# The first attention of a decoder layer with one product of query and key weights instead of two projections

## The chip, the cores and the metric

The kernel runs on one core of one Trainium2 chip. The core has five engines that run their own streams of instructions and meet at semaphores: TensorE (matmuls, PE in the profile), VectorE (DVE), ScalarE (ACT), GpSimd (POOL) and SyncE (SP), which here issues DMA transfers. The metric is the device time of one execution of the whole kernel in microseconds; lower is better. SBUF is the memory on the chip that the engines read; PSUM holds what TensorE writes, in 8 banks.

## What is computed

A decoder layer over x of 4 batches of 512 rows and 256 columns: a causal attention with one head, a second attention with 16 heads whose keys and values come from a context, and a mixture of 8 experts; each adds to its input and is followed by a layer norm. The part that the change touches is the first attention:

```python
q = x @ Wq + bq
k = x @ Wk + bk
v = x @ Wv + bv
att = jnp.einsum('bqd,bkd->bqk', q, k) * scale
att = jnp.where(causal, -jnp.inf, att)
att = jax.nn.softmax(att, axis=-1)
out = jnp.einsum('bqk,bkd->bqd', att, v)
return out @ Wo + bo
...
x = _layernorm(x + _L0_attn_ref(x, ...), axis=-1)
x = _layernorm(x + _L0_xattn_ref(x, ctx_1024, ctx_1024, ...), axis=-1)
x = _layernorm(x + _L0_ffn_ref(x, ...), axis=-1)
```

## The kernel before

All data is float32. Where accuracy matters, a factor is kept as two parts, high and low (`lo_of` makes the low one), and a product is three matmuls (`mm3`, L239): high by high, high by low, low by high. In names, `a_s` is the split transposed x, `c_s` the split transposed context, `W_s` the split weights, `k_s` and `q_s` the keys and queries of the second attention on their way to DRAM, `X` the rows of the residual, `ps` the PSUM.

A batch is 4 tiles of 128 rows (NT) and two blocks of 128 columns (KD). The work goes in bodies, one for each batch b; body 0 and body 3 are written out, 1 and 2 are one loop (Fori) on every engine. A body is: `half`, the scores of the second attention of batch b for one half of the heads; `glue_and_attention1`, which ends the batch b - 1 (g) and computes the whole first attention of batch b + 1 (n); the other `half`; and `project2`, the projections of batch b + 1 for the second attention. A prologue brings in the weights and does the first attention of batch 0. After the bodies come the shared MLP, the routing, the experts and the last norm, from about 390 us on. Each engine runs its instructions in the order in which they are written; semaphores (`s["name"]`) alone tie the engines together.

In the glue (by the lines of the profile) TensorE runs: keys of the first attention, `projected` 0 and 1 (12 matmuls of 128x512, L239 `a_s,w_s`); aug transposes (L1355); transposes of the outputs, `turn_out` (L1600); queries, `projected` 2 and 3; behind cb_out the rows of values times output weights, `rows_of(0, ...)` (24 of 128x256); the turn of the second attention's combined output (L1336); scores of the first attention (L239 `c_s,q_s`, with a mask matmul L1418); the output projection of the second (24 of 128x256, `w_s,a_s`, whose `a_s` now holds the turned output); transposes of the probabilities (L1428); and PV (30 of 128x256, `v_s,pT_s`). VectorE runs the aug operations (L1071 to L1079), the copies and low parts, `combine` (L1104 to L1115, which reads the PSUM banks of the outputs, and counts cb_out), `maximum` (L981), `residual2` (L938) and `turned` (low parts of pT_s, L865). ScalarE makes the exponents and the high parts. GpSimd splits x and the context (L401 the high part, L404 the low one) and adds the bias to the values of the second attention (`v_aug`, L485). The raw context lies in `c_raw`, which also holds the values that L485 reads (`v_wait`); so SP loads the next context behind v_set, at the end of its queue of stack loads (`q_stack<-augT` L300, `k_stack<-k_rows` L283, twelve `q_stack<-q_rows` L294, `c_raw` L330).

## Time and profile before

| | us |
|---|---|
| three runs | 865.03, 865.67, 866.78 |
| median | 865.67 |
| profiled execution | 866.4 |
| its span, from the first to the last instruction | 864.6 |
| TensorE busy | 770.9 (89%) |
| VectorE, ScalarE, GpSimd busy | 404.8, 354.7, 240.6 |

The mean granted clock of TensorE is 0.957 of its upper level, 2.4 GHz. The prologue ends at 53 us; the glues stand at 66 to 88 us (body 0), 142 to 169 (body 1), 224 to 251 (body 2), 306 to 323 (body 3); the last body's work ends at about 390.

A timeline row reads: start, busy time, engine, line, operation, written tensor <- read tensors, form, and how many of one kind stand there; in brackets the engine's idle time ahead and what ended it. PE rows are matmuls, PEld rows the loads of their stationary factor, which overlap them.

### The profile page before, as it was taken

How to read it: one execution, taken by the hardware profiler on the slowest of the kernel's cores; microseconds unless marked ns; L12 is line 12 of the kernel's file. 1: busy time of each engine (PE TensorE's matmuls, PEld its weight loads, DVE VectorE, ACT ScalarE, POOL GpSimd, SP SyncE). 2: the span in 40 equal slices, each digit the busy share in tenths (PEclk: the TensorE clock that was granted, in tenths of full speed). 3: DMA queues.
4: the chain of work that ended last, by engine and by line, in shares of the span. 5: the costliest groups of instructions: out<-in, count | busy, mean ns of one | idle time of the engine just before them, and what ended most of it. 6: DMA issues, size and time to landing. Idle time of an engine off the chain costs nothing. (4 is left out here: it accounts for less than half of the span.)

```text
span 864.6 us, 15341 instructions
## 1 busy us (share of the span) xinstructions
PE 770.9 (89%) x4898; PEld 584.7 (68%) x4899; DVE 404.8 (47%) x763; ACT 354.7 (41%) x914; POOL 240.6 (28%) x262
## 2 busy tenths in 40 slices
PE   6889999899999989964899989999999999999920
PEld 4757676867777666554899966677677667767710
DVE  4565877687768757235744522122212212221216
ACT  2223655366546726604544303433433343343313
POOL 5860231141123012023277751111111111111116
PEclk9988999999999999985999999999999999999975
DMA  9945041404312440007511164410010101111034
GB/s 298 203 135 101 1 138 28 75 6 133 64 36 56 154 77 1 5 1 249 209 55 55 56 176 164 150 36 30 30 36 30 36 31 36 30 30 36 19 138 165
DMA packets 54292, 71.57 MB, mean 83 GB/s; under 512 B 14992, under 2 KB 40464, under 8 KB 53360
## 3 DMA queue, kind: packets, MB, share of 16 engines
q1 hardware_dynamic: 50848, 61.75, 26.4%
q0 software_dynamic: 3408, 9.34, 3.0%
q8 instruction: 23, 0.38, 0.2%
q14 instruction: 13, 0.11, 0.0%
HBM read 47.67 MB, written 22.88 MB: 82 GB/s over the span
## 5 line engine op out<-in xcount | busy, mean ns | idle before, releaser
L1745 PE MATMUL ps<-we,hT 128*128 x624 | 142.8, 382 | 2.5 <-ACT hT L819 2.5
L1745 PEld LDWEIGHTS ps<-we,hT 128*128 128x128 f32 x624 | 119.7, 192 | 35.5 <-issue 20.9
L1725 PE MATMUL ps<-we,xT 128*128 x312 | 140.6, 593 | 1.9 <-issue 1.9
L1263 DVE COPY hp<-ps 128x512 f32<-128x512 f32 x78 | 50.3, 686 | 158.4 <-PE ps L1725 158.4
L1059 DVE TENSOR_REDUCE mx<-ps 128x4 f32<-128x512 f32 (+1 forms) x128 | 103.9, 821 | 30.6 <-PE ps L1557 29.1
L819 ACT ACTIVATE hT<-ps,b1T 128x128 f32<-128x128 f32 x312 | 85.3, 386 | 35.1 <-PE ps L1736 35.1
L1725 PEld LDWEIGHTS ps<-we,xT 128*128 128x128 f32 x312 | 56.2, 190 | 58.1 <-issue 58.1
L607 ACT ACTIVATE xT<-ps 128x256 f32<-128x256 f32 x39 | 15.0, 386 | 180.4 <-PE ps L1708 180.4
L1557 PE MATMUL ps<-k_stack,q_stack 96*128 96x256 f32 (+1 forms) x256 | 73.1, 372 | 5.6 <-issue 1.7
L721 ACT ACTIVATE pT<-ps 128x256 f32<-128x256 f32 x128 | 49.4, 386 | 61.2 <-PE ps L1573 52.3
L583 POOL CAST yidx<-meta 128x1 int32 (+1 forms) x39 | 7.2, 185 | 238.5 <-ACT yw L828 238.5
L1557 PEld LDWEIGHTS ps<-k_stack,q_stack 96*128 96x128 f32 x256 | 40.4, 199 | 33.8 <-issue 23.2
L724 ACT ACTIVATE pT<-ps 128x256 f32<-128x256 f32 (+1 forms) x128 | 62.5, 489 | 0.0
L1271 DVE TENSOR_TENSOR ysum<-ps,b2b 128x256 f32<-128x256 f32 x39 | 16.6, 425 | 95.2 <-PE ps L1745 95.2
L239 PE MATMUL ps<-xT_s,ws_s 128*128 128x256 f32 x384 | 49.6, 291 | 11.0 <-DVE xT_s L865 9.2
L239 PEld LDWEIGHTS ps<-xT_s,ws_s 128*128 128x128 f32 x384 | 48.6, 200 | 11.7 <-issue 11.7
L239 PE MATMUL ps<-ws_s,h_s 128*128 128x256 f32 x384 | 47.9, 284 | 0.0
L239 PEld LDWEIGHTS ps<-ws_s,h_s 128*128 128x128 f32 x384 | 46.5, 191 | 0.5 <-DVE ws L1183 0.5
L586 POOL DMA_INDIRECT pair_out<-yw,yidx x39 | 38.3, 983 | 29.6 <-POOL yidx L583 29.6
L1579 PE MATMUL ps<-q_stack,k_stack 98*128 98x256 f32 (+1 forms) x128 | 46.3, 362 | 0.0
L1736 PE MATMUL ps<-ident,hp 128*128 128x128 f32 x312 | 40.5, 273 | 1.4 <-DVE hp L1263 1.4
L239 PE MATMUL ps<-a_s,w_s 128*128 128x512 f32 x144 | 38.1, 412 | 2.9 <-DVE a_s L865 1.5
(221 smaller groups left out, 1202.0 us busy)
## 6 DMA issues: line engine op xcount, KB each, us to landing
we<-in_w SPq DMA_DIRECT2D x16, 1024.0 KB
k_stack<-k_rows SPq DMA_DIRECT2D x24, 256.0 KB, 4.8
slot_rows<-attn SPq DMA_DIRECT2D x1, 4992.0 KB, 25.0
xs<-slot_rows SPq DMA_DIRECT2D x39, 128.0 KB, 2.0
k_rows<-k_s SPq DMA_DIRECT2D x16, 256.0 KB, 3.1
yl<-pair_out SPq DMA_DIRECT2D x4, 1024.0 KB, 8.8
q_stack<-q_rows SPq DMA_DIRECT2D x48, 64.0 KB, 5.7
x_raw<-in_xT SPq DMA_DIRECT2D x4, 512.0 KB, 5.5
```

Source lines behind the costliest of these rows:

```text
L239: m = nc.tensor.matmul(out, lhs(a), rhs(b), start=first and n == 0, stop=last and n == 2, skip_group_check=check)
L586: pool.indirect_dma_start(out=pair_out, out_offset=bass.IndirectOffsetOnAxis(ap=yidx[:, q, :], axis=0), in_=yw[:, q, :], in_offset=None).t ...
L721: nc.scalar.activation(pT[:, m % 2, u % 2, 0:2 * P], ps[:, bank, 256:512], ACT.Exp, scale=SCALE2)\
L724: nc.scalar.activation(pT[:, m % 2, u % 2, 2 * P:2 * P + w], ps[:, bank + 1, 0:w], ACT.Exp, scale=SCALE2).then_inc(s["b_exp"], 1)
L819: last = nc.scalar.activation(hT[:, c, :], ps[:, 4 + c // 4, (c % 4) * P:(c % 4 + 1) * P], ACT.Gelu, bias=b1T[:, bass.ds(e * NH + c, 1)])
L1059: nc.vector.tensor_reduce(mx[:, n, 2 * p:2 * p + 2, r0:r0 + nb], ps[:, 2 * ((u + flip) % 2):2 * ((u + flip) % 2) + 2, 0:nb * P].rearrange( ...
L1263: last = nc.vector.tensor_copy(hp[:, c * 512:(c + 1) * 512], ps[:, 2 + c, :])
L1557: m = nc.tensor.matmul(ps[:, 2 * ((u + flip) % 2) + j, 0:nb * P], q_stack[0:96, ha * HALF + PAIRS * j + p, n * P:(n + 1) * P], k_stack[0:9 ...
L1579: nc.tensor.matmul(ps[:, bank + 1, 0:w].rearrange("p (h n q) -> p h n q", h=2, q=P), k_stack[0:98, p, i * P:(i + 1) * P], qv[0:98, :, :].r ...
L1725: m = nc.tensor.matmul(ps[:, 2 + c, :], xT[:, q, k, :], w[:, bass.ds(e, 1), k * HID + c * 512:k * HID + (c + 1) * 512].rearrange("p o n -> ...
L1736: m = nc.tensor.transpose(ps[:, 4 + c // 4, (c % 4) * P:(c % 4 + 1) * P], hp[:, c * P:(c + 1) * P], ident[:, :])
L1745: m = nc.tensor.matmul(ps[:, 6, 0:D], hT[:, c, :], w[:, bass.ds(e, 1), KD * HID + c * D:KD * HID + (c + 1) * D].rearrange("p o n -> p (o n)"),
```

## The change

Scores are x (Wq Wk^T) x^T plus terms of the biases. The product M = Wq Wk^T is formed once in the prologue on TensorE (4 matmuls of 128x256 in float32), scaled and split; the host hands over Wq and Wk transposed for it. Each batch then projects only once (`projected` 0 and 1, into `y_s`, which shares memory with k_s), and the keys of the scores are x itself, `a_s`. The turned output of the second attention goes into `at_s` (memory of q_s) instead of a_s, and its writer waits until q_s has gone to DRAM. The term that is constant over a query's row, x u + a scalar with u = Wq bk, is not in the scores; it is a column `shift`, made by `shifts` on VectorE (multiply 128x1024, reduce, add) for the batch after the next one, and each row maximum goes through one more 128x1 operation that subtracts it and adds it again. In the loop shifts stand ahead of turned(2). (A constant that is left out of a row's scores does not change its softmax.)

GpSimd: the split of batch 0's x goes to ScalarE and VectorE; c_s of batch 0 is split ahead of W_s[1]; in the bodies c_s's split waits for v2_ps of this batch instead of w1_ps of the next; v_aug's addition waits for cb_out as well. One memset of k_stack moves from VectorE to GpSimd, and SP's first loads come in another order (Wq and Wk first, then x, biases, Wv and Wo, X of batch 0, the context, the second attention's weights, the rest).

```diff
@@ SBUF
+        u_row = sb("u_row", [P, D], F, att)
+        shift = sb("shift", [P, B * NT], F, att)
+        shift0 = sb("shift0", [P, 2], F, att)
+        at_s = q_s
+        y_s = k_s
+        xu = x_raw[:, :, :].rearrange("p k t -> p (k t)").rearrange("p (n d) -> p n d", n=NT)
-        q1_s = sb("q1_s", [P, 2, KD, S], FR, att)
@@ GpSimd, prologue
-            split(a_s, x_raw, (("x_raw_in", 16),), "xa_hi", "xa_lo", 0)
+            split(c_s, c_raw, (("c_raw_in", 16),), "ctx_hi", "ctx_lo", 0)
             pool.wait_ge(s["w2_in"], 16 * 4)
...
-            split(c_s, c_raw, (("s1_ps", NT), ("c_raw_in", 16)), "ctx_hi", "ctx_lo", 0)
@@ GpSimd, body
                 if not first:
                     pool.wait_ge(s["pv_done"], 8 * 2 * b)
+                    pool.wait_ge(s["cb_out"], 2 * b)
                 pool.wait_ge(s["v2_out"], 2 * b + 2)
...
-                    split(c_s, c_raw, (("w1_ps", 2 * b + 4), ("c_raw_in", 16 * b + 32)), "ctx_hi", "ctx_lo", b + 1)
+                    split(c_s, c_raw, (("v2_ps", 2 * b + 2), ("c_raw_in", 16 * b + 32)), "ctx_hi", "ctx_lo", b + 1)
@@ ScalarE, glue_and_attention1
-                    act.wait_ge(s["qk1_ps"], 4 * n + j + 1)
-                    copy_bias((c_s, q1_s)[j // 2][:, 0, j % 2, :], ps[:, 4 + j, :],
-                              bcol[:, 1 - j // 2, j % 2:j % 2 + 1], "qk1_hi")
+                    act.wait_ge(s["qk1_ps"], 2 * n + j + 1)
+                    copy_bias(y_s[:, 0, j, :], ps[:, 4 + j, :], bcol[:, 0, j:j + 1], "qk1_hi")
...
-                    copy(a_s[:, 0, :, :], ps[:, 2:4, :], "at_hi")
+                    copy(at_s[:, 0, :, :], ps[:, 2:4, :], "at_hi")
@@ VectorE, prologue
+            lo_of(a_s[:, 1, :, :], x_raw[:, :, :], a_s[:, 0, :, :], "xa_lo")
+            dve.wait_ge(s["m_ps"], 1)
+            m_hi = W_s[0][:, 0, 0, :, :].rearrange("p k n -> p (k n)")
+            nc.vector.tensor_scalar(m_hi, ps[:, 2, :], SCALE1, None, ALU.mult).then_inc(s["w1_hi"], 1)
...
+            def shifts(b, at, first=False):
+                col = shift[:, bass.ts(b, NT)]
+                nc.vector.tensor_tensor(xu, X[:, bass.ts(b, NT), :], u_row[:, :].unsqueeze(1).broadcast_to([P, NT, D]), ALU.mult)\
+                    .then_inc(s["shift_step"], 1)
+                dve.wait_ge(s["shift_step"], at + 1)
+                nc.vector.tensor_reduce(col, xu, AX, ALU.add).then_inc(s["shift_step"], 1)
+                dve.wait_ge(s["shift_step"], at + 2)
+                nc.vector.tensor_scalar(col, col, shift0[:, 0:1] if first else shift0[:, 1:2], None, ALU.add)\
+                    .then_inc(s["shift_step"], 1)
@@ VectorE, maximum(i)
                     nc.vector.tensor_reduce(nmax[:, i:i + 1], ps[:, 4 + i, 0:(i + 1) * P], AX, ALU.max, negate=True)\
-                        .then_inc(s["s1_max"], 1)
+                        .then_inc(s["s1_raw"], 1)
+                    dve.wait_ge(s["s1_raw"], NT * n + i + 1)
+                    col = shift[:, bass.ds(NT * n + i, 1)]
+                    nc.vector.scalar_tensor_tensor(out=nmax[:, i:i + 1], in0=nmax[:, i:i + 1], scalar=col, in1=col,
+                                                   op0=ALU.subtract, op1=ALU.add).then_inc(s["s1_max"], 1)
@@ TensorE, prologue
+                        for i in range(KD):
+                            for k in range(KD):
+                                m = nc.tensor.matmul(ps[:, 2, i * D:(i + 1) * D], raw1[:, 0, k, i * P:(i + 1) * P],
+                                                     raw1[:, 1, k, :], start=k == 0, stop=k == KD - 1)
+                        m.then_inc(s["m_ps"], 1)
@@ TensorE, glue_and_attention1
-                    projected(2)
-                    projected(3)
+                    rows_of(6, a_s, w, 2, "v1_ps")
                 if g is not None:
                     pe.wait_ge(s["cb_out"], 2 * g + 2)
-                if n is not None:
-                    rows_of(0, a_s, w, 2, "v1_ps")
...
+                        if i >= 2:
+                            pe.wait_ge(s["v1_lo"], 2 * n + i - 1)
                         for k in range(KD):
-                            m = mm3(pe, ps[:, 4 + i, 0:wd], lambda l: q1_s[:, l, k, i * P:(i + 1) * P],
-                                    lambda l: c_s[:, l, k, 0:wd], k == 0, k == KD - 1)
+                            m = mm3(pe, ps[:, 4 + i, 0:wd], lambda l: y_s[:, l, k, i * P:(i + 1) * P],
+                                    lambda l: a_s[:, l, k, 0:wd], k == 0, k == KD - 1)
```

How this stands on the engines. TensorE, glue in the loop, from the first projection to the scores (rows that only repeat a form are left out). Before:

```order
L239 MATMUL ps<-a_s,w_s 128x512 [waits s_xa_lo]
...
L1355 MATMUL ps<-ident,aug 32x128 [waits s_aug_ready]
...
L1600 MATMUL ps<-ident,oT 128x128 [waits s_os_out,s_oc_out]
...
L1600 MATMUL ps<-ident,oT 128x128 [waits s_augT_out]
...
L239 MATMUL ps<-a_s,w_s 128x512 [waits s_os_out,s_oc_out]
...
L239 MATMUL ps<-w_s,a_s 128x256 [waits s_cb_out]
L239 MATMUL ps<-w_s,a_s 128x256 x23
L1336 MATMUL ps<-ident,attn 128x128 x8
```

After:

```order
L245 MATMUL ps<-a_s,w_s 128x512 [waits s_xa_lo]
...
L1406 MATMUL ps<-ident,aug 32x128 [waits s_aug_ready]
...
L1665 MATMUL ps<-ident,oT 128x128 [waits s_os_out,s_oc_out]
...
L1665 MATMUL ps<-ident,oT 128x128 [waits s_augT_out]
...
L245 MATMUL ps<-w_s,a_s 128x256 [waits s_os_out,s_oc_out]
...
L1387 MATMUL ps<-ident,attn 128x128 [waits s_cb_out]
...
L245 MATMUL ps<-a_s,k_s 128x256 [waits s_qk1_lo]
```

The second projection is gone, the 24 matmuls of the v rows stand where it stood and wait for oc_out and os_out, and cb_out is waited for by the attention turn.

VectorE, the same glue, from the last maxima to the reciprocal of the denominators. Before:

```order
L981 TENSOR_REDUCE nmax<-ps 128x1 [waits s_s1_ps]
L865 TENSOR_TENSOR pT_s<-ps,pT_s 128x256 [waits s_pt_hi]
L938 ISA [waits s_w2_ps,s_x_kept]
L938 TENSOR_TENSOR res<-ps,X 128x512
L938 ISA [waits s_w2_ps]
L938 TENSOR_TENSOR res<-ps,X 128x512
L865 TENSOR_TENSOR pT_s<-ps,pT_s 128x384 [waits s_pt_hi]
L865 TENSOR_TENSOR pT_s<-ps,pT_s 128x512 [waits s_pt_hi]
L1005 RECIPROCAL den<-den 128x4 [waits s_s1_exp]
```

After:

```order
L1024 TENSOR_REDUCE nmax<-ps 128x1 [waits s_s1_ps]
...
L1028 SCALAR_TENSOR_TENSOR nmax<-nmax,shift 128x1
L886 TENSOR_TENSOR pT_s<-ps,pT_s 128x256 [waits s_pt_hi]
L980 ISA [waits s_w2_ps,s_x_kept]
...
L980 TENSOR_TENSOR res<-ps,X 128x512
...
L910 TENSOR_TENSOR x_raw<-X,u_row 128x1024
...
L913 TENSOR_REDUCE shift<-x_raw 128x4
...
L915 TENSOR_SCALAR shift<-shift 128x4 [waits s_shift_step]
L886 TENSOR_TENSOR pT_s<-ps,pT_s 128x384 [waits s_pt_hi]
L886 TENSOR_TENSOR pT_s<-ps,pT_s 128x512 [waits s_pt_hi]
L1056 RECIPROCAL den<-den 128x4 [waits s_s1_exp]
```

A chained 128x1 operation stands behind each maximum, and the three operations of shifts ahead of the last two of turned.

GpSimd, the loop's body from x's low part to the context's split. Before:

```order
L404 TENSOR_TENSOR a_s<-x_raw,a_s 128x1024 [waits s_xa_hi]
L484 ISA [waits s_pv_done]
L485 TENSOR_TENSOR v_aug<-c_raw,brow 128x64x16 [waits s_v2_out]
L400 REGISTER_ALU
L401 TENSOR_TENSOR c_s<-c_raw,zero 128x1024 [waits s_c_raw_in,s_w1_ps]
L404 TENSOR_TENSOR c_s<-c_raw,c_s 128x1024 [waits s_ctx_hi]
```

After:

```order
L416 TENSOR_TENSOR a_s<-x_raw,a_s 128x1024 [waits s_xa_hi]
L498 REGISTER_ALU [waits s_pv_done]
L499 REGISTER_ALU [waits s_cb_out]
L500 TENSOR_TENSOR v_aug<-c_raw,brow 128x64x16 [waits s_v2_out]
L413 TENSOR_TENSOR c_s<-c_raw,zero 128x1024 [waits s_c_raw_in,s_v2_ps]
L416 TENSOR_TENSOR c_s<-c_raw,c_s 128x1024 [waits s_ctx_hi]
```

The order is the same; v_aug waits for cb_out besides, and the context's split for v2_ps instead of w1_ps.

## Rows read from the trace of the kernel before

**Rows 1.** Page, parts 1 and 2: busy time, and the clock in 40 slices.

```profile
PE 770.9 (89%) x4898; PEld 584.7 (68%) x4899; DVE 404.8 (47%) x763; ACT 354.7 (41%) x914; POOL 240.6 (28%) x262
...
PEclk9988999999999999985999999999999999999975
```

**Rows 2.** Timeline of body 1: start us, busy us, engine, line, operation, [idle, releaser].

```profile
142.61 2.59 PEld L239 LDWEIGHTS ps<-a_s,w_s 128*128 128x128 f32 x12 [0.20 <-issue]
...
142.88 2.40 POOL L485 TENSOR_TENSOR v_aug<-c_raw,brow 128x1024 f32<-128x1024 f32 x1 [13.71 <-PE ps L1531]
143.00 2.36 DVE L1079 TENSOR_TENSOR aug<-dloc,aug 128x32 fp32r<-128x32 f32 x1
...
145.42 0.36 PEld L1355 LDWEIGHTS ps<-ident,aug 128*32 128x32 f32 x4 [0.21 <-DVE aug L1079]
...
146.06 1.73 PEld L1600 LDWEIGHTS ps<-ident,oT 128*128 128x128 f32 x16 [0.28 <-issue]
...
151.70 2.94 PEld L239 LDWEIGHTS ps<-w_s,a_s 128*128 128x128 f32 x24 [1.36 <-DVE attn L1115]
...
155.51 0.41 SPq L330 DMA_DIRECT2D c_raw<-in_cT  x1
...
163.55 0.68 DVE L981 TENSOR_REDUCE nmax<-ps 128x1 f32<-128x512 f32 x1
...
165.49 3.66 PEld L239 LDWEIGHTS ps<-v_s,pT_s 128*128 128x128 f32 x30
...
165.72 0.55 DVE L865 TENSOR_TENSOR pT_s<-ps,pT_s 128x384 fp32r<-128x384 f32 x1
...
169.07 0.31 PEld L1557 LDWEIGHTS ps<-k_stack,q_stack 96*128 96x128 f32 x2
...
169.44 1.89 POOL L401 TENSOR_TENSOR c_s<-c_raw,zero 128x1024 fp32r<-128x1024 f32 x1 [24.15 <-PE ps L239]
...
171.41 2.36 POOL L404 TENSOR_TENSOR c_s<-c_raw,c_s 128x1024 fp32r<-128x1024 f32 x1
```

**Rows 3.** Timeline of body 3, the same place.

```profile
306.09 2.34 DVE L1077 CAST aug<-dloc 128x32 fp32r<-128x32 f32 x1
...
308.73 0.91 PE L1355 MATMUL ps<-ident,aug 128*32 128x128 f32 x4 [2.85 <-DVE aug L1079]
309.37 3.15 PEld L1600 LDWEIGHTS ps<-ident,oT 128*128 128x128 f32 x16 [0.21 <-issue]
```

**Rows 4.** Windows in which last bytes moved: busy by engine, PEclk, DMA share, GB/s.

```profile
124.00:124.25 0.25, 0.17 (x1) 0.17 (x1) 0.25 (x2) 0.25 (x2) 0.00 (x0) 1.00 0.31 115
160.00:160.25 0.25, 0.25 (x4) 0.25 (x4) 0.00 (x0) 0.00 (x0) 0.00 (x0) 1.00 0.05 16
242.00:242.25 0.25, 0.25 (x5) 0.25 (x4) 0.00 (x0) 0.00 (x0) 0.00 (x0) 1.00 0.23 82
```

**Rows 5.** Groups by form, VectorE: count, busy us, mean ns, idle before.

```profile
L865 DVE TENSOR_TENSOR ws_s<-ws,ws_s 128x2048 fp32r<-128x2048 f32 x1 | 2.3, 2291 | 2.6 <-ACT ws_s L607 2.6
...
L1076 DVE TENSOR_TENSOR aug<-ncross,aug 128x32 fp32r<-128x32 f32 x8 | 1.7, 217 | 0.3
```

**Rows 6.** Timeline of body 0, the first projection.

```profile
66.40 4.25 PEld L239 LDWEIGHTS ps<-a_s,w_s 128*128 128x128 f32 x12
```

**Rows 7.** Timeline of body 1, GpSimd behind x_raw's landing.

```profile
124.82 1.89 POOL L401 TENSOR_TENSOR a_s<-x_raw,zero 128x1024 fp32r<-128x1024 f32 x1 [13.76 <-DMA x_raw<-in_xT]
```

**Rows 8.** Windows with TensorE's granted clock (PEclk).

```profile
57.00:66.00 9.00, 8.26 (x20) 4.70 (x19) 7.84 (x11) 0.00 (x0) 6.55 (x3) 0.50 0.00 0
310.00:312.00 2.00, 2.00 (x12) 2.00 (x11) 0.00 (x0) 0.44 (x2) 0.00 (x0) 0.50 0.05 13
```

**Rows 9.** Timeline of the prologue: SP's issues and TensorE's start of the half.

```profile
18.20 14.26 SPq L264 DMA_DIRECT2D slot_rows<-pad_end  x1
...
41.95 3.08 SPq L270 DMA_DIRECT2D k_rows<-k_s  x2
...
53.03 0.83 PE L1557 MATMUL ps<-k_stack,q_stack 96*128 96x256 f32 x4 [1.75 <-issue]
```

More of the change, by code:

```diff
@@ L150, in build @@
         turned.close()
-        q1_s = sb("q1_s", [P, 2, KD, S], FR, att)
+        sb("turned", [P, 2, 2, S], F, att)
         att.close()
@@ L884, in _ @@
+            dve.wait_ge(s["x0_in"], 16)
+            shifts(0, 0, True)
             dve.wait_ge(s["wvo_ps"], 1)
@@ L965, in glue_and_attention1 @@
                     projected(1)
+                    if g is None and not first:
+                        dve.wait_ge(s["xbo"], B)
+                        dve.wait_ge(s["xa_lo"], n + 1)
+                        shifts(n, 3 * n + 2)
                 if g is not None:
@@ L1001, in glue_and_attention1 @@
                 if n is not None:
+                    if not first:
+                        dve.wait_ge(s["x_kept"], kept)
+                        dve.wait_ge(s["xa_lo"], n + 1)
+                        shifts((n + 1) % B, 3 * (n + 1) + 2)
                     turned(2)
```

134 lines of the change are left out of this document (80 added, 54 removed).

## The prediction

> **What bounds the kernel now.** I read the page first: TensorE is busy 89% of the span, and its granted clock is at its upper level nearly everywhere [rows 1]. So in the three stages that the change touches (prologue, four glues, second attention's start) the question is what TensorE does or waits for. Then I read the timeline of the glue in body 1 [rows 2], where all engines can be followed, and the same place in body 3 [rows 3]. The chain that ended last is of no use here: it covers only the end of the span, which nothing in this change reaches. After 390 us the same work stands in the same order, so whatever is gained or lost before shifts the end one for one.
>
> What the reader is to see in [rows 2]: TensorE projects queries and keys (12 weight loads in 2.59 us), waits for VectorE's aug, which is late because its last operation took 2.36 us beside GpSimd's 2.40 us v_aug addition; then runs transposes (16 in 1.73) and the second projection, and its loads stand 1.36 us before the v rows, whose banks the combine holds until L1115. Later, PV starts at 165.49 and the next half at 169.07. GpSimd's split of c_s starts only at 169.44, behind w1_ps, though the last bytes of c_raw moved just after 160.0 [rows 4].
>
> All sums are against the profiled execution, 866.4 us (span 864.6). The median of the runs is 865.67, 0.73 lower; I take that off at the end.
>
> **TensorE's work.** Per batch the second projection goes: 12 matmuls of 128x512, 2.59 us by the first projection's row [rows 2]. The v rows go into banks 6 and 7, so they no longer wait for the combine; they run under it. The aug wait ends sooner too, since v_aug's addition now waits for cb_out. In body 1 aug's transposes follow the first projection at 145.20 rather than at 145.42, and of the 0.28 us of issue behind that wait some 0.24 is covered too: 0.46 less (bound: 0.22). Then 16 transposes (to 147.3), 24 v rows (to 150.2), and the attention turn when the combine has ended, at 151.70 - 0.46 = 151.24. Before, the v rows started there and took 2.88 (24 weight loads in 2.94 [rows 2], less what the next overlaps) ahead of that turn. So everything from there on is 0.46 + 2.88 = 3.34 us earlier: max(3) starts at 163.55 - 3.34 = 160.21 and ends at 160.89. Without a new wait each loop body would gain 3.3.
>
> **VectorE's work.** Each maximum gets a chained 128x1 operation with two inputs in SBUF; the trace has none so small. The 128x32 ones with two SBUF inputs take 0.22 [rows 5], and from below the bound is zero, overlapped with the maximum's tail; I take 0.1, and since maxima 0 to 2 run ahead of need, only the last one lies on the path. The three operations of shifts stand between residual2 and turned(2). The multiply (128x1024, both inputs in SBUF): 2.29 us is one of 128x2048 [rows 5], so 1.15 to 1.37; I take 1.22. The reduction of 1024: max(3), one of 512, takes 0.68 [rows 2], so at most 1.36; I take 1.22. The 128x4 addition 0.2. With gaps 2.75 us. turned(2) now follows max(3) by 1.49 us (164.23 to 165.72 [rows 2], with turned(1) and residual2 between), and PV needs it for its last 21 of 30 matmuls. PV has 3.58 us, so 9 matmuls are 1.07 and 21 are 2.50.
>
> **Body 0.** It has no aug stall (its aug is ready under the half-clock projection, 4.25 us [rows 6]). Gain 2.65 of matmuls; loss 2.75 behind shifts, of which about 1.3 lies past the 9 matmuls and the wait for exponents; +0.3 for chained operations and clock. Net -1.0 to -0.7; I take **-0.7**.
>
> **Bodies 1 and 2: who has the port.** The split of c_s (L401 1.89, L404 2.36 [rows 2]) now waits only for c_raw and v2_ps. c_raw is issued at the end of SP's queue of stack loads, which starts with augT: 0.46 earlier. Its last bytes moved at about 160.03 in body 1, and in body 2 at 242.12, which is 160.47 on body 1's scale (81.65 apart) [rows 4]. x_raw's last bytes at 124.2 released GpSimd at 124.82, 0.6 later [rows 4, 7]. So c_s starts at 160.03 + 0.6 - 0.46 = 160.17 in body 1 and 160.6 in body 2. VectorE asks for its chained 128x1 at 160.93. GpSimd is there first, by 0.76 and 0.33 us. In [rows 2] the 128x32 operation asked 0.12 us behind L485 and ended when that did, and in [rows 3] a cast did the same (2.34 for what is otherwise 0.19). So the 128x1 ends at 162.15. exp(3) follows it. turned(1) and residual2 read PSUM and end about 163.7. The multiply then asks, finds L404 (162.14 to 164.50), and starts at 164.5; shifts end at 167.3, turned(2) at 167.85, PV's 21 matmuls at 170.35 against 169.07: **+1.3**. In body 2, with everything 0.43 later, **+1.7**. If VectorE asked first, the split's first part would run from about 161.0 to 162.95, the multiply behind it, turned(2) to 166.4, PV to 168.9: -0.2.
>
> The Trainium skill, "SBUF — State Buffer", section "Who interferes with whom", says that a VectorE instruction with two SBUF inputs contends with a GpSimd instruction that reads SBUF, and that whoever issues first keeps the shared pair for the whole instruction. The two blocked rows agree. It also says that a tensor_reduce never contends on trn2, which no row here shows; by it the reduction of shifts could not be held, which my sum does not assume either way. Were the port shared in turns instead, the 128x1 would cost 0.1 and both bodies would stand near -0.2.
>
> **Clock.** TensorE would stand idle about 2.2 us before pT's last transposes and 3 us within PV. What such a wait does: in body 3 an idle of 2.85 us [rows 3] was followed by transposes at 3.15 instead of 1.73 us, and the window 310 to 312 shows 0.50, the lower level [rows 8]. A spell costs 1.42 there; with 21 matmuls of PV under it, up to 2.5 and more. Other waits of 1 us left the clock up. I take one spell over the two bodies, **+1.4** (none to two, 0 to 2.8).
>
> **Body 3.** No batch follows, so no projection is saved there; but L485 moves behind the combine. L1077 (2.34) and L1079 then take 0.2 each, aug is ready at about 306.6 instead of 308.7, and the transposes run at the upper clock: -2.1 - 1.4 = **-3.5**, all of it on the path, since combine, Wo and the next half follow in a chain. Bound: the query stack's loads have their own pace, which no row here times; if they hold the half, -2.5 is the other end.
>
> **Prologue.** The product adds 4 matmuls, two bias rows and a column, replaces two splits by one, and makes batch 0's projection 12 matmuls shorter. TensorE ends its work at 51.28 before (53.03 less the idle) and then stands 1.75 us, until 53.03; the key rows were issued at 41.95 but could not move before slot_rows' pads (issued from 18.20 for 14.26 us), and the key stack follows from them [rows 9]. Up to 3 us earlier or 1.7 later on TensorE change nothing there: **0**, bounds -1 and +2.
>
> **Sum.** -0.7 + 1.3 + 1.7 + 1.4 - 3.5 + 0 = +0.2: 866.6 by the profiled run, **865.9** by the median.
>
> **The rivals.** (A, forecast) both bodies blocked, one spell; without it 864.5, with two 867.3. For it: two blocked rows and the order of arrival; against it: margins of 0.33 and 0.76 us rest on a landing time that I could be wrong on by as much.
> (B, faster) VectorE is first in one or both bodies, or the loads land later. One: -0.7 + 1.3 - 0.2 - 3.5, with or without a spell, 862.6 to 864.0; both: -4.6, 861.1. For it: c_raw moves behind twelve stack loads on the same queue, and need not come earlier by all that its issue does.
> (C, slower) the stall is the one forecast, but the lower clock stays on as it did from 57 to 66 us (9 us at 0.50 [rows 8]) after the 1.75 us of idle at 53.03. Then each of two spells holds PV and the start of the half, 2.5 instead of 0.7: +3.6 on top, 869.5; one of them long, 868. It decides from the point where more than 1.5 us beyond A's is lost to clock. Against it: the half-clock at 310 ended within 3 us.
> (D) the full gain shows: shifts hide and nothing blocks: -2.6 - 3.3 - 3.3 - 3.5 = -12.7, 853. Against it, PV needs turned(2), which stands behind 2.75 us of new work.
> (E) the product does not do what it says: the prologue's new chain (product, split, shifts) outlasts the loads and costs 2 us or more, 867.9.
>
> **Chances.** A 0.40, B 0.30, C 0.20, D 0.05, E 0.05. About 0.2%, 1.7 us, is what a measurement can tell from no change. Faster than 863.9: B nearly whole, D, a little of A, 0.35. Slower than 867.4: C, E, A's upper edge, 0.28. Between: 0.37. The range runs from B's lower end, 861.1, to between C's two values, 869.3; D and C's tail are left out. A's own range is 864.5 to 867.3.
>
> **What the changed kernel's profile would show.** Scores start 3.3 us earlier in body 1; L485's successor starts behind the combine and no aug operation is over 0.3 us; a 128x1 operation of 1.2 us (body 1) or 1.6 (body 2) beside GpSimd's c_s, and a multiply that waits 0.8 behind the second part; idle TensorE of 3 us within the PV matmuls, and a clock below 1 behind it; body 3's transposes at 1.73; the first half still starting at 53.0. I am wrong if the 128x1 operations are all short (B), if the clock row shows slices under 9 from 160 to 260 us (C), or if the half in body 0 starts over 2 us early (D).

## The result and the profile after

The changed kernel takes 869.0 us (median of six executions, 866.24 to 870.31), the kernel before 864.98 beside it: 1.0035 times as long (95% interval 1.0020 to 1.0049). In a second set of runs it was 866.94 against 864.31, 1.0022 (1.0005 to 1.0040). By these ratios it is 0.2 to 0.35% slower, 2 to 3 us (the medians of the two pairs lie 4.0 and 2.6 us apart), though TensorE runs 36 matmuls of 128x512 less from body 0 to body 2 alone. The profiled execution is the shortest of the first six: 866.24 us, span 864.5, beside 866.4 and 864.6 before. That one trace therefore shows less than the median's loss; a second one is below.

The page's rows on TensorE and its clock, for [rows 1]:

```profile
PE 767.2 (89%) x4874; PEld 582.0 (67%) x4875; DVE 413.4 (48%) x789; ACT 349.1 (40%) x907; POOL 240.8 (28%) x261
...
PEclk9988999899989999985999999999999999999975
```

3.7 us less busy, and the clock is below 9 tenths in more slices: 8 at the eighth, 8 at the twelfth. There lie the glues of bodies 1 and 2.

To find where the time goes I compare marks in two timelines: the start of each `half` and of each glue (the first weight load of each). From one mark to the next the kernels run the same stage, so the change of the difference between marks is what the stage costs or gives. I use the same marks for every kernel below. All in us against the trace before, a plus is later; "body 0" runs from the first half's start to the second's and holds the first glue; "body 3" runs from the end of glue 2 to the end of the last glue (323 us before the change). Each row is one execution.

| kernel | start of first half | body 0 | glue 1 | glue 2 | body 3 | sum, at 323 us |
|---|---|---|---|---|---|---|
| changed, first trace | -0.17 | -1.62 | +1.97 | +3.48 | -3.58 | +0.09 |
| changed, second trace (after_again) | +3.76 | -0.98 | +2.23 | +0.56 | -3.53 | +2.06 |
| shift_early | +1.41 | +0.06 | -2.76 | -2.81 | -3.59 | -7.70 |
| cs_late | -0.41 | -1.00 | +0.88 | +1.29 | -3.61 | -2.75 |
| no_cb_wait | +0.20 | -1.13 | +4.31 | +4.05 | -0.14 | +7.43 |
| pre_order | +3.21 | -1.10 | +1.95 | +1.18 | -3.37 | +1.83 |
| warm_pv | +2.12 | -1.03 | +2.72 | +2.96 | -3.58 | +3.16 |
| before_cb | -1.41 | +0.13 | -0.19 | -0.23 | -3.60 | -5.36 |
| early_pre | +5.41 | +0.65 | -2.76 | -2.79 | -3.61 | -3.18 |
| early_bcol | +0.86 | +1.37 | +0.44 | -1.49 | -3.66 | -2.58 |
| no_shift | -0.11 | -2.66 | -3.10 | -3.16 | -3.61 | -12.74 |
| no_shift_bcol | +0.59 | -2.28 | -3.12 | -3.15 | -3.61 | -11.61 |
| early_but_body0 | +1.90 | -0.42 | -2.76 | +0.20 | -3.60 | -4.74 |

(The stages between, projections and later halves, differ by 0.12 at most and are left out.)

Glue 1 of the changed kernel, for [rows 2] (its timeline stands 1.77 us earlier at the start):

```profile
140.84 2.59 PEld L245 LDWEIGHTS ps<-a_s,w_s 128*128 128x128 f32 x12 [0.20 <-issue]
...
141.22 0.21 DVE L1130 TENSOR_TENSOR aug<-dloc,aug 128x32 fp32r<-128x32 f32 x1
...
145.77 2.94 PEld L245 LDWEIGHTS ps<-w_s,a_s 128*128 128x128 f32 x24
...
153.45 0.41 SPq L342 DMA_DIRECT2D c_raw<-in_cT  x1
...
158.66 0.68 DVE L1024 TENSOR_REDUCE nmax<-ps 128x1 f32<-128x512 f32 x1
...
159.47 0.22 DVE L1028 SCALAR_TENSOR_TENSOR nmax<-nmax,shift 128x1 f32<-128x1 f32 x1
...
159.74 1.89 POOL L413 TENSOR_TENSOR c_s<-c_raw,zero 128x1024 fp32r<-128x1024 f32 x1 [7.52 <-DMA c_raw<-in_cT]
...
161.13 1.58 DVE L910 TENSOR_TENSOR x_raw<-X,u_row 128x1024 f32<-128x1024 f32 x1
...
161.71 3.21 POOL L416 TENSOR_TENSOR c_s<-c_raw,c_s 128x1024 fp32r<-128x1024 f32 x1
162.86 1.22 DVE L913 TENSOR_REDUCE shift<-x_raw 128x1024 f32 x1
164.12 0.83 DVE L915 TENSOR_SCALAR shift<-shift  x1
...
165.45 3.89 PEld L245 LDWEIGHTS ps<-v_s,pT_s 128*128 128x128 f32 x21 [3.06 <-DVE pT_s L886]
...
169.27 0.31 PEld L1622 LDWEIGHTS ps<-k_stack,q_stack 96*128 96x128 f32 x2
```

Read against [rows 2]. Aug's last operation takes 0.21 us, the v rows start at 145.77, behind the transposes and beside the combine, and the last maximum stands at 158.66, 17.82 us behind the start of the projection where it was 20.94: 3.12 earlier. Then comes what takes it back. VectorE goes through the chained operation (159.47), the multiply (161.13), the reduction and the addition before turned(2), and the last 21 matmuls of PV start at 165.45 after 3.06 us of idle, ended by `DVE pT_s L886`. These 21 take 3.89 us, not 2.5. The clock had fallen ahead of that wait, while the nine matmuls before it ran: 0.63 from 161.5 to 162.0, and 0.50 from there to 168. The next half stands at 28.43 us behind the projection, before at 26.46.

Glue 2, the same place, in the first trace and in the second, with the clock under PV in each (window, busy by engine, PEclk, DMA share, GB/s):

```profile
242.88 1.89 POOL L413 TENSOR_TENSOR c_s<-c_raw,zero 128x1024 fp32r<-128x1024 f32 x1 [7.06 <-DMA c_raw<-in_cT]
243.07 1.72 DVE L1028 SCALAR_TENSOR_TENSOR nmax<-nmax,shift 128x1 f32<-128x1 f32 x1
...
246.24 2.06 DVE L910 TENSOR_TENSOR x_raw<-X,u_row 128x1024 f32<-128x1024 f32 x1
...
250.44 4.03 PEld L245 LDWEIGHTS ps<-v_s,pT_s 128*128 128x128 f32 x21 [3.14 <-DVE pT_s L886]
```

```profile
248.00:250.00 2.00, 0.00 (x0) 0.00 (x0) 1.82 (x4) 0.00 (x0) 0.00 (x0) 0.50 0.00 0
```

```profile
254.00:256.00 2.00, 2.00 (x18) 2.00 (x19) 1.34 (x4) 0.00 (x0) 0.00 (x0) 1.00 0.00 0
```

```profile
247.92 0.22 DVE L1028 SCALAR_TENSOR_TENSOR nmax<-nmax,shift 128x1 f32<-128x1 f32 x1
...
248.12 1.89 POOL L413 TENSOR_TENSOR c_s<-c_raw,zero 128x1024 fp32r<-128x1024 f32 x1 [7.46 <-DMA c_raw<-in_cT]
...
253.83 2.57 PEld L245 LDWEIGHTS ps<-v_s,pT_s 128*128 128x128 f32 x21 [3.31 <-DVE pT_s L886]
```

In the first trace GpSimd's split began at 242.88 and the chained 128x1 operation of VectorE, which asked 0.19 us later, took 1.72 us instead of 0.22 and ended with it; the multiply, held by the split's second part, took 2.06 instead of 1.22. PV's last 21 matmuls waited 3.14 and took 4.03. In the second trace VectorE was first by 0.20 us, its 128x1 took 0.22, and though the weight loads stood for 3.31 us, the clock was at its upper level behind that (1.00 from 254 to 256): the 21 took 2.57. The same code, 2.9 us apart.

Body 3, for [rows 3]:

```profile
309.73 0.19 DVE L1128 CAST aug<-dloc 128x32 fp32r<-128x32 f32 x1
...
310.23 0.61 PE L1406 MATMUL ps<-ident,aug 128*32 128x128 f32 x4 [0.69 <-DVE aug L1130]
...
310.87 1.73 PEld L1665 LDWEIGHTS ps<-ident,oT 128*128 128x128 f32 x16 [0.31 <-issue]
```

The cast takes 0.19 us where it took 2.34, aug's transposes wait 0.69 instead of 2.85, and the sixteen transposes' weight loads 1.73 instead of 3.15: they run at the upper clock.

The prologue is where the two traces of the changed kernel part. First trace, then second (for [rows 9]):

```profile
4.39 3.78 PE L1425 MATMUL ps<-oT 128*128 128x256 f32 x8 [4.39 <-DMA oT<-in_L_attn_Wk]
9.01 1.13 PE L1430 MATMUL ps<-oT,bcol 128*128 128x256 f32 x4 [0.84 <-DMA brow<-in_brow]
...
11.23 3.57 PE L1443 MATMUL ps<-oT 128*128 128x256 f32 x8
...
25.69 1.80 DVE L1028 SCALAR_TENSOR_TENSOR nmax<-nmax,shift 128x1 f32<-128x1 f32 x1
...
52.95 0.76 PE L1622 MATMUL ps<-k_stack,q_stack 96*128 96x256 f32 x4
```

```profile
9.89 2.07 PE L1430 MATMUL ps<-oT,bcol 128*128 128x256 f32 x4 [1.65 <-DMA brow<-in_brow]
...
14.17 3.76 PE L1443 MATMUL ps<-oT 128*128 128x256 f32 x8
```

TensorE forms the product, then waits for the biases (`brow` ended the wait): 0.84 us in one execution, 1.65 in the other. The bias rows then took 1.13 and 2.07 us, the rest up to the first projection longer too; the projection starts at 15.41 and at 19.08, and the first half at 52.95 and at 56.88 (-0.17 and +3.76 in the table). Twice the length for the same matmuls looks like the lower clock, which the first trace does show a little later (0.50 from 12 to 14 us), but the second does not confirm it: its clock reads 1.00 from 9 to 14 us. Nor does the length of the wait decide. In the trace of warm_pv, which has the same prologue:

```profile
9.57 1.13 PE L1430 MATMUL ps<-oT,bcol 128*128 128x256 f32 x4 [1.67 <-DMA brow<-in_brow]
```

It waited 1.67 us and the rows took 1.13; shift_early waited 1.25 and they took 2.08; early_bcol below took 1.91 with no wait at all. What decides is open. A second loss is plain in the first trace: the chained 128x1 operations of batch 0 run beside GpSimd's split of the weights (L449) and its addition to X (L454, 25.13 to 27.48), and three of them take 0.95, 0.87 and 1.80 us instead of 0.22.

### The profile page after: what moved, and what is told of

Read it like the earlier page. It is cut to its first block and busy times, and to the rows that moved or that the text cites. A ratio compares the mean times of both kernels' runs of the same rounds, so it can differ in the third digit from the quotient of the medians.

```text
span 864.5 us, 15342 instructions
## 1 busy us (share of the span) xinstructions
PE 767.2 (89%) x4874; PEld 582.0 (67%) x4875; DVE 413.4 (48%) x789; ACT 349.1 (40%) x907; POOL 240.8 (28%) x261
## 5 line engine op out<-in xcount | busy, mean ns | idle before, releaser
L1638 PE MATMUL ps<-q_stack,k_stack 100*128 100x256 f32 x128 | 38.8, 304 | 0.8 <-DVE logits L1066 0.3
```

Of the source, the lines that this page charges most:

```text
L1638: nc.tensor.matmul(ps[:, bank, 256:512].rearrange("p (h q) -> p h q", h=2), k_stack[0:100, p, i * P:(i + 1) * P], qv[0:100, :, i * P:(i + ...
```

## The experiments

Each is the changed kernel with the edit shown, but for before_cb. Each ratio is to the kernel before, run beside it.

**after_again**: no edit, a second trace of the changed kernel.

> The changed kernel as it is, for a second trace. Its profiled execution took 866.2 us, the lowest of its six, while the median is 869.0. If what sets an execution apart is how long TensorE stays at its lower clock behind the idle in PV (162 to 169 and 247 to 253 us in the first trace, at 0.50), a trace of an execution near 869 shows the same instructions, the same two spells or longer ones, and 2 to 3 us more in stretches at 0.50. The rival: the extra lies where before and after run the same work (from 390 us on), and the glue looks the same in both traces.

Measured: 866.94 us, 1.0022 (1.0005 to 1.0040); profiled 868.07. The extra was in neither of the two places named: glue 2 even had no spell at the lower clock. It was in the prologue (+3.76), and glue 2 gave most of that back. The rival, the later stages, is out too: from 323 us on both traces keep their distance to the kernel before within 0.4 us.

**shift_early**: shifts under the output projection.

```diff
                     maximum(2)
+                    if not first:
+                        dve.wait_ge(s["x_kept"], kept)
+                        dve.wait_ge(s["xa_lo"], n + 1)
+                        shifts((n + 1) % B, 3 * (n + 1) + 2)
                     turned(0)
...
-                    if not first:
-                        dve.wait_ge(s["x_kept"], kept)
-                        dve.wait_ge(s["xa_lo"], n + 1)
-                        shifts((n + 1) % B, 3 * (n + 1) + 2)
                     turned(2)
```

> Only shifts moves: from ahead of turned(2) to behind the third maximum, where VectorE stood idle for 3.1 us in bodies 1 and 2. Theory 1, the stall in PV is the price of the change: the 2.8 us of idle and the lower clock on 21 matmuls (1.4 us) go in both bodies, so that with 3.3 us saved each the kernel takes 854 to 857 us. In body 0 shifts costs about 0.5 there. Theory 2, the price is the port, held by GpSimd's earlier split of c_s: the last chained 128x1 operation is still blocked for up to 1.5 us in one or both bodies, exp(3) and the rest follow it, 857 to 861. A third: the median stays above 863, and neither is the cause.

Measured: 861.36 us, 0.9963 (0.9951 to 0.9974); the profiled execution 859.54. Both bodies turned from a loss of 2 to 3.5 us into a gain of 2.8 each. Glue 1:

```profile
158.68 1.23 DVE L910 TENSOR_TENSOR x_raw<-X,u_row 128x1024 f32<-128x1024 f32 x1
...
162.74 0.22 DVE L1028 SCALAR_TENSOR_TENSOR nmax<-nmax,shift 128x1 f32<-128x1 f32 x1
...
162.98 1.90 POOL L413 TENSOR_TENSOR c_s<-c_raw,zero 128x1024 fp32r<-128x1024 f32 x1 [7.47 <-DMA c_raw<-in_cT]
...
164.24 3.84 PE L245 MATMUL ps<-v_s,pT_s 128*128 128x256 f32 x30
```

The multiply takes 1.23 us, the 128x1 operation 0.22, since it stands 0.24 us ahead of the split, and PV's 30 matmuls run in one piece at the upper clock. So theory 1 holds for the mechanism. Its number (854 to 857) was too low: it left out the prologue (+1.41 here) and took too little for body 0, where shifts has no cover (+0.06 instead of -1.6, with the lower clock under PV, whose 30 matmuls took 5.33 us there and 3.84 before), and it took the last 128x1 operation to be free of the port in every execution, which early_bcol below shows it is not.

**cs_late**: the context's split behind w1_ps again.

```diff
-                    split(c_s, c_raw, (("v2_ps", 2 * b + 2), ...), "ctx_hi", "ctx_lo", b + 1)
+                    split(c_s, c_raw, (("w1_ps", 2 * b + 4), ...), "ctx_hi", "ctx_lo", b + 1)
```

> Only the split of c_s moves back behind w1_ps, so GpSimd is idle while VectorE runs the last maximum and shifts. Theory 1: the blocked pieces go (1.0 us in body 1, 2.3 us in body 2), but shifts still stands ahead of turned(2), TensorE still idles about 1.8 us in PV, and the lower clock may still follow: 864 to 867 us. Theory 2, the port is the price: 856 to 860 us, near what the 12 matmuls of each batch promised.

Measured: 863.57 us, 0.9992 (0.9979 to 1.0005), just under the range of theory 1, and 3.4 us under the changed kernel's 866.94 of the same set. Glue 1:

```profile
161.52 1.21 DVE L910 TENSOR_TENSOR x_raw<-X,u_row 128x1024 f32<-128x1024 f32 x1
...
164.87 4.08 PE L245 MATMUL ps<-v_s,pT_s 128*128 128x256 f32 x21 [2.21 <-DVE pT_s L886]
```

Multiply and addition take 1.21 and 0.23 us (1.58 and 0.83 in the changed kernel), the idle in PV is 2.21 instead of 2.77, the clock is down all the same. Against the changed kernel's first trace the moved split costs 1.1 us in glue 1 and 2.2 in glue 2, against the second 1.4 and -0.7, since here the clock was down in glue 2 and there it was not; the stall that stays, with the clock under it, costs 3.6 to 4.1 (cs_late against shift_early).

**no_cb_wait**: v_aug's addition does not wait for the combine.

```diff
                     pool.wait_ge(s["pv_done"], 8 * 2 * b)
-                    pool.wait_ge(s["cb_out"], 2 * b)
```

> Only the wait of v_aug's addition for cb_out is taken out again. It stands beside the aug operations as before the change. If this wait alone gave body 3 its 3.5 us (aug operations free, transposes at the upper clock) and 0.46 us in bodies 1 and 2, the kernel takes 872 to 874 us, and body 3 shows an aug operation of 2.3 us. If body 3's gain came from elsewhere, it stays at 869.

Measured: 872.94 us, 1.0095 (1.0069 to 1.0121). Body 3 is back to -0.14:

```profile
313.56 2.37 POOL L499 TENSOR_TENSOR v_aug<-c_raw,brow 128x1024 f32<-128x1024 f32 x1 [30.46 <-PE ps L1595]
313.64 2.34 DVE L1127 CAST aug<-dloc 128x32 fp32r<-128x32 f32 x1
...
316.29 1.03 PE L1405 MATMUL ps<-ident,aug 128*32 128x128 f32 x4 [2.85 <-DVE aug L1129]
```

The cast is again 2.34 us beside GpSimd's 2.37, aug's transposes wait 2.85 and take 1.03. This wait alone gives body 3's 3.5 us. In glues 1 and 2 the kernel lost 2.3 and 0.6 us against the changed kernel's first trace, 2.1 and 3.5 against the second, where 0.46 each was expected. Its trace shows what came on top:

```profile
160.56 1.82 DVE L1027 SCALAR_TENSOR_TENSOR nmax<-nmax,shift 128x1 f32<-128x1 f32 x1
```

GpSimd's split had begun at 160.47, in glue 2 at 246.52 with the 128x1 operation 0.12 us behind it (1.79 us): both bodies were blocked as I had forecast for the changed kernel. TensorE then idled 2.6 us ahead of the last transposes, and the clock was down from 163 to 172 and from 248 to 258. VectorE asks 18.86 us behind the projection here and 18.63 in the changed kernel, so the aug wait that comes back (0.23 us) is enough to turn an order that was decided by 0.2 to 0.3 us; one trace does not show that it does so each time.

**before_cb**: the kernel before with that one wait.

```diff
                     pool.wait_ge(s["pv_done"], 8 * 2 * b)
+                    pool.wait_ge(s["cb_out"], 2 * b)
```

> The kernel before with one part of the change alone: v_aug's addition waits for cb_out as well. Aug's operations are no longer beside it: body 3 gains 3.5 us (2.1 of wait, 1.4 of lower clock), bodies 1 and 2 about 0.4 each: 860 to 861 where the kernel before has 864.3 to 865. If the wait holds SP's queue or the context's split up instead, 864 or more.

Measured: 860.66 us, 0.9958 (0.9943 to 0.9973): body 3 -3.60, glues 1 and 2 -0.19 and -0.23. One line added to the kernel before is worth 3.6 us, and the changed kernel hides it, since its own -3.6 in body 3 is in the table too.

**warm_pv**: TensorE kept busy in PV's wait.

```diff
                     for i in range(NT):
+                        if i == 2 and g is not None:
+                            keep_clock(12, bank=7)
                         pe.wait_ge(s["pt_lo"], NT * n + i + 1)
```

> The changed kernel with 12 matmuls of 128x512 into an unused bank (2.6 us) in the idle ahead of the last 21 matmuls of PV, in bodies 1 and 2. The stall stays, only TensorE is not idle in it. If the lower clock is part of the price, the 21 matmuls take 2.5 us instead of 3.9 to 4.1 and the kernel gains 1.4 per spell: 865 to 867.5 where the changed one has 867 to 869. If the stall alone is the price, the time stays as it is or rises by up to 0.5.

Measured: 867.72 us, 1.0038 (1.0024 to 1.0052): no gain. Glue 1:

```profile
162.36 1.43 DVE L1028 SCALAR_TENSOR_TENSOR nmax<-nmax,shift 128x1 f32<-128x1 f32 x1
...
164.67 1.11 PE L1493 MATMUL ps<-ident,pT 128*128 128x128 f32 x4 [2.19 <-ACT pT L664]
...
167.50 3.16 PE L1382 MATMUL ps<-w_s 128*128 128x512 f32 x12
...
170.27 2.69 PEld L245 LDWEIGHTS ps<-v_s,pT_s 128*128 128x128 f32 x21
```

The 21 matmuls do run at the upper clock (2.69 us), but in this trace the lower one had come earlier, behind the 2.2 us that TensorE waited for the blocked 128x1 operation: the transposes at 164.67 took 1.11 instead of 0.66 and the first 12 filler matmuls 3.16. The spell moved, it did not go. What the clock costs by itself can be read elsewhere: 3.89 to 4.07 against 2.57 us for the same 21 matmuls in the traces of the changed kernel, 1.3 to 1.5 (1.4 forecast), in one or two of the two bodies.

**pre_order**: both weight products first, then the bias rows.

```diff
+                        pe.wait_ge(s["w1_in"], 32)
+                        for i in range(KD):
...
+                        m.then_inc(s["wvo_ps"], 1)
                         pe.wait_ge(s["bias_in"], 32)
...
-                        pe.wait_ge(s["w1_in"], 32)
-                        for i in range(KD):
...
-                        m.then_inc(s["wvo_ps"], 1)
```

> The changed kernel with another order in the prologue alone: TensorE forms the product of the value and output weights right behind that of query and key weights, and only then the bias rows, whose loads landed at 9.0 to 9.9 us while TensorE stood idle for 0.8 to 1.7 us; VectorE makes the first shifts behind these. Theory: that idle and the lower clock behind it are what moved the first half's start by +3.8 us in one trace of the changed kernel and by -0.2 in another; without it the start stays near 52.8 in every execution, the median falls by 2 to 3 us to 864 to 866, and executions lie closer together. Rival: the first half waits for the slot_rows and k_rows transfers in any case, and the median stays at 867 to 869.

Measured: 869.6 us, 1.0063 (1.0043 to 1.0084): a miss. TensorE then waited for Wo instead, and longer, and later for y_s, since the biases' scaling stood behind more work:

```profile
10.94 2.89 PE L1431 MATMUL ps<-oT 128*128 128x256 f32 x8 [2.92 <-DMA oT<-in_L_attn_Wo]
...
25.35 1.50 PE L245 MATMUL ps<-a_s,k_s 128*128 128x256 f32 x6 [2.03 <-DVE k_s L889]
```

So the wait for brow was not special: it ends at 9.0 to 9.9 us in the traces of the unedited prologue, the wait for Wo at 10.9 here and at 11.8 in early_pre, and TensorE stands until the one that it needs next has landed. By the ratios the kernel is 2.4 and 3.5 us slower than the changed one was in its two sets; its first half at +3.21 alone would not show that, since the unedited prologue gave -0.17 to +3.76.

**early_pre**: the edits of shift_early and of pre_order together.

> shift_early and pre_order together. The two parts are in different stages, so they should add: shift_early's 861.4 less 2 to 3 us, 858 to 860. If they share the waits for the first half's key stack, it stays at 861.

Measured: 863.66 us, 1.0006 (0.9985 to 1.0026). The glues are those of shift_early (-2.76, -2.79), the first half starts 5.41 us late. The parts add, with pre_order's sign.

**early_bcol**: shift_early, with the small biases ahead of x.

```diff
+            sp.dma_start(bcol..., bcol_d).then_inc(s["bias_in"], 16)
             sp.dma_start(x_raw..., xT_d...).then_inc(s["x_raw_in"], 16)
-            sp.dma_start(bcol..., bcol_d).then_inc(s["bias_in"], 16)
-            sp.dma_start(brow..., brow_d...).then_inc(s["bias_in"], 16)
+            sp.dma_start(brow..., brow_d...).then_inc(s["x0_in"], 16)
...
-                        pe.wait_ge(s["bias_in"], 32)
+                        pe.wait_ge(s["bias_in"], 16)
```

> shift_early with the biases of bcol loaded ahead of x and TensorE waiting for them alone, not for the broadcast of brow as well. Theory: the idle between the weight product and the bias rows (0.8 to 1.7 us) and the lower clock behind it go, the first half starts near 52.5 in every execution, and 861.4 becomes 859 to 860. If the bias loads are late for another reason, or the later stages wait for the stack loads anyway, it stays at 861.4.

Measured: 861.91 us, 0.9952 (0.9936 to 0.9967), beside shift_early's 0.9963: no difference that counts.

```profile
7.97 1.91 PE L1430 MATMUL ps<-oT,bcol 128*128 128x256 f32 x4
...
53.89 0.83 PE L1622 MATMUL ps<-k_stack,q_stack 96*128 96x256 f32 x4 [1.69 <-issue]
```

```profile
163.48 1.93 DVE L1028 SCALAR_TENSOR_TENSOR nmax<-nmax,shift 128x1 f32<-128x1 f32 x1
163.50 1.89 POOL L413 TENSOR_TENSOR c_s<-c_raw,zero 128x1024 fp32r<-128x1024 f32 x1 [7.26 <-DMA c_raw<-in_cT]
...
166.27 0.66 PE L1493 MATMUL ps<-ident,pT 128*128 128x128 f32 x4 [2.69 <-ACT pT L664]
```

The idle at the product is gone, but the bias rows are slow all the same (1.91 us). TensorE is ready 1.69 us before the first half starts, so as before the change something else sets that start; that it is the stack's transfers is argued from the order of the loads, the row itself says only `issue`. And glue 1 shows what shift_early's trace had been spared: VectorE's 128x1 operation and GpSimd's split stand 0.02 us apart, and the operation takes 1.93 us. TensorE waits 2.69 and the glue is at +0.44 instead of -2.76. In glue 2 GpSimd was ahead by 0.37 us, the operation took 1.53, and the glue is at -1.49.

**no_shift**: the row constant left out: no shifts, no chained operation, no row of u. The softmax is the same in exact arithmetic; the rounding of the exponent's argument is not.

```diff
                     nc.vector.tensor_reduce(nmax[:, i:i + 1], ..., ALU.max, negate=True)\
-                        .then_inc(s["s1_raw"], 1)
-                    dve.wait_ge(s["s1_raw"], NT * n + i + 1)
-                    nc.vector.scalar_tensor_tensor(out=nmax[:, i:i + 1], ...)
+                        .then_inc(s["s1_max"], 1)
...
-                        shifts((n + 1) % B, 3 * (n + 1) + 2)
```

> The changed kernel without the row constant: no shifts, no chained operation behind the maxima, and no row of u in the prologue (mathematically the softmax is the same; what is left out is how the exponent is rounded). It prices the row constant: bodies 1 and 2 gain 3.3 us each against the kernel before and body 0 2.6 to 2.9, with body 3's 3.5 that makes 12.7 us, less 1 to 3 for the prologue: 853 to 855. If the split of c_s or the lower clock costs by itself, without shifts, 857 or more.

Measured: 854.26 us, 0.9863 (0.9846 to 0.9880). Every glue gains 3.1 to 3.3 (the one of body 0, taken alone, 3.29), body 3 its 3.6:

```profile
158.16 1.89 POOL L413 TENSOR_TENSOR c_s<-c_raw,zero 128x1024 fp32r<-128x1024 f32 x1 [6.93 <-DMA c_raw<-in_cT]
...
159.62 3.84 PE L245 MATMUL ps<-v_s,pT_s 128*128 128x256 f32 x30
```

PV runs in one piece although GpSimd's split starts at 158.16, ahead of it, and the last two low parts of VectorE keep their 0.55 and 0.69 us beside it: without the row constant's operations the split costs nothing that can be seen. This version beats both kernels; 3.6 us of its gain are before_cb's one wait.

**no_shift_bcol**: no_shift with the loads' edit of early_bcol.

> no_shift with bcol ahead of x as in early_bcol. The prologue's idle goes: 1 to 2 us below no_shift, 851.5 to 854. If the prologue is limited by the transfers of slot_rows and k_rows, no difference.

Measured: 853.96 us, 0.9861 (0.9846 to 0.9876), no difference to no_shift.

**early_but_body0**: early_bcol with body 0's shifts where the change had them.

```diff
                     maximum(2)
-                    if not first:
+                    if not first and g is not None:
...
                         shifts((n + 1) % B, 3 * (n + 1) + 2)
                     turned(0)
...
+                    if not first and g is None:
...
+                        shifts((n + 1) % B, 3 * (n + 1) + 2)
                     turned(2)
```

> early_bcol, but in body 0 shifts stays where the change put it (ahead of turned(2)). In body 0 there is no output projection under which VectorE idles, so the early place delays turned(0), the last maximum and all that follows: its glue took 0.5 to 1.4 us more than before the change with the early place and 0.7 to 1.1 less with the late one. Expected: body 0's glue at -0.7 to -1.1 against the kernel before and the whole kernel 1.2 to 2 us below early_bcol, a ratio near 0.9935 to the kernel before. If the stall there matters as in bodies 1 and 2, no gain.

Measured: 862.38 us, 0.9946 (0.9927 to 0.9964). Body 0 improves as expected (-0.42 instead of +1.37, its glue alone -0.76), the whole by too little to tell from early_bcol. Glue 1 is at -2.76, glue 2 at +0.20:

```profile
241.54 1.93 DVE L1028 SCALAR_TENSOR_TENSOR nmax<-nmax,shift 128x1 f32<-128x1 f32 x1
241.57 1.89 POOL L413 TENSOR_TENSOR c_s<-c_raw,zero 128x1024 fp32r<-128x1024 f32 x1 [7.29 <-DMA c_raw<-in_cT]
```

Again a tie, 0.03 us apart, that VectorE lost. So as long as the chained operation is there and the split is early, shifts' early place leaves a body at -2.8, at -1.5 or near nothing, by a few tenths of a microsecond in who comes first.

## Why the prediction was right or wrong

The time fell into the stated range (861.1 to 869.3), 1 to 3 us above the 865.9 forecast. Against the kernel before it is 1.9 and 3.0 us slower by the ratios, more than the 1.7 that I took as the least to tell, and so on the slower side, to which I had given 0.28, less than to the other two. By its own steps:

**Body 3**: forecast -3.5, measured -3.58 and -3.53, and no_cb_wait and before_cb show the cause to be the one named.

**Bodies 1 and 2**: forecast +1.3 and +1.7 with +1.4 for one spell of the lower clock, 4.4 together. Measured 5.45 in one trace and 2.79 in the other. That the mean of the two, 4.1, comes out near 4.4 is partly luck, as the steps below show. The saving upstream was forecast at 3.34 a body and is 3.1 to 3.2 (no_shift): the attention turn came 0.22 us earlier by the aug wait, my bound, and not 0.46. The place of the stall (turned(2) behind shifts, 21 matmuls of PV waiting) and its idle of 3 us (2.77 to 3.24 between matmuls) were right, and shift_early shows that it was the main price. The way there was partly wrong. I let the 128x1 operation be blocked in both bodies; it was in one glue of the four that the two traces show, and there the sizes came out: 1.72 us for the operation (1.6 forecast), +3.48 for the body with its spell (1.7 and 1.4 forecast). In the other three VectorE was first, by 0.20 to 0.33 us. The step that failed is the arrival: I moved c_raw's landing with its issue, from body 1 of the kernel before. It was issued at 153.45, its last bytes moved between 159.00 and 159.25, and GpSimd began at 159.74: the 0.6 between the last two is as I had taken it, but 5.7 us passed from the issue to the last bytes where I had 4.5 ([rows 2, 4]). Body 2 of the kernel before, issued at 236.29 and done at 242.12, shows 5.8, which my sum did not use. VectorE's side was late too, by 0.3 us, mostly from the smaller saving upstream. So rival B's condition held (the loads land later), yet not its gain, because other pieces were blocked instead: the multiply by the end of the split's first part (1.50 to 1.65 us instead of 1.22), and the 128x4 addition, at 0.2 in my sum, by its second part (0.83). Such a body without a spell is at +0.56 (glue 2 of the second trace), where my case for VectorE first had -0.2. I had weighed the port for the operations that start ahead of shifts and left out the small one at its end. The chained operation itself costs 0.36 us on the path where I took 0.1: TensorE's idle ahead of the last transposes is 0.98 us instead of 0.62.

**Clock**: one spell over the two bodies was forecast; the first trace had two (162 to 168, 247 to 254), the second one, at 170 to 174, in glue 1 only. The price of 1.4 on 21 matmuls was right. The sign that I had named for C came up, slices under 9 between 160 and 260 us, in the eighth and the twelfth slice; yet C, a spell that holds the next half too, did not occur: the two ended at 168.5 and 253.8, ahead of the halves at 169.27 and 254.41. The sign could not tell C from two short spells. And the wait in PV is not the whole cause of a spell, since in both glues of the first trace the clock fell ahead of it, while the nine matmuls ran.

**Body 0**: forecast -0.7, measured -1.62 and -0.98. The glue alone gave -1.13 and -0.71, near the forecast; the rest lies in the half ahead of it, which I had not counted. TensorE idled 0.91 us in PV where I took 1.3 to be lost, and the last chained operation cost some 0.26 (0.88 us of idle ahead of the last transposes instead of 0.62).

**Prologue**: this is the term that was mis-sized. Forecast 0, with bounds of -1 and +2. In the six traces of kernels with the changed prologue as it is the first half starts at -0.17, +3.76, +1.41, -0.41, +0.20 and +2.12 (mean +1.15); in the two with the old one at 0 and -1.41. That is some 1.9 us on average and up to 4 in one execution. I had argued that the key stack's transfers set the start and that TensorE had 1.75 us to spare. What failed is that margin: in the two traces of the changed kernel TensorE has no idle left ahead of the first half, and where it has some (2.61 us in no_shift, 1.69 in early_bcol, 1.92 in early_but_body0) the half starts at -0.11, +0.86 and +1.90, so what else sets the start moves as well. Two things used the margin up. The chained operations of batch 0 are held by GpSimd (0.95, 0.87 and 1.80 us): in the first trace the scores start 0.96 us earlier than before the change, at 21.23, and PV 0.95 later, at 30.18. And the matmuls ahead of the first projection take either of two lengths, which with the 0.8 us of longer wait puts the two traces 3.7 us apart at 19 us; what decides is open, since it is not whether TensorE waited for the biases, or how long. Rival E (0.05, 867.9) was this, the new chain outlasting the loads, and had far too small a chance.

**The total**: by the means of these traces, -1.3 in body 0, +4.1 in glues 1 and 2, -3.6 in body 3 and +1.9 in the prologue make +1.1 us; by the two ratios the runs say +1.9 and +3.0. Some 1 to 2 us stay open. So the range held with one term mis-sized by as much as the whole effect; executions of the changed kernel spread over 7 us (863.4 to 870.2), those of the kernel before over 4, and two traces are few for that. The gain of rival D, -12.7, is what the trace of no_shift shows at 323 us, -12.74.

On the port, the Trainium skill ("SBUF — State Buffer", "Who interferes with whom") says that issue order decides who blocks and that the first keeps the shared pair for the whole instruction. Where GpSimd stood ahead, by 0.09 to 0.47 us (glue 2 of the changed kernel, no_cb_wait, warm_pv), VectorE waited until the first part had ended; where VectorE was ahead by 0.14 to 0.33 (the changed kernel's other glues, shift_early, early_pre), it did not, and so far the traces agree. In the ties, 163.48 and 163.50, 241.54 and 241.57, VectorE waited though its start is recorded first, so to hundredths the record does not tell who has the port. The section also says that a tensor_reduce never contends; here the reduction of shifts, which reads SBUF, takes 1.22 us beside GpSimd's second part (162.86 above) as it does alone (at 248.45 in glue 2), so the trace agrees.

## What to carry to other kernels

Work saved on the bounding engine is gained only if what takes its place on the other engines has a cover of its own: look for the stretch in which the helper engine idles (here 3.1 us under the output projection) and put the new step there, not in front of the last steps of the chain. A VectorE operation on the path that reads SBUF twice, however small, can last until the GpSimd operation that it meets has ended (1.82 us for one of 0.22); either keep GpSimd still there or take the operation out. And when one change bundles several edits, time each alone: here one added wait was worth 3.6 us by itself, and the algebra was worth 9 only without the constant that came with it.

## What was not expected of the hardware

A VectorE tensor_scalar of 128x4, with one input in SBUF, took 0.83 us beside GpSimd's split (0.23 alone) and ended with it, as the cast of [rows 3] had; so not only operations with two SBUF inputs are held. GpSimd's operations are lengthened too: L416 took 3.21 us instead of 2.37 where it met the multiply. The clock did not follow one wait in a fixed way. In both glues of the changed kernel's second trace and in glue 1 of the first, TensorE did the same work up to PV, idled 0.71 and 0.98 us around pT's transposes, ran nine matmuls and then idled some 3 us. Once the clock fell under the nine matmuls, ahead of the long idle (between 161.5 and 162.0); once behind the idle (between 170.0 and 170.5); once not at all (1.00 from 248 to 258). What would settle the ties, shifts early with the context's split late, was not run: in it the last chained operation should meet nothing.
